# Result rows of a routed feed-forward added to the output by accumulating DMAs, in place of a read-back and sums on chip

## The reference

```python
x = x + tanh(g_xattn) * xattn(ctx, layernorm(x), mask, mask, ...)   # 8 heads, 16 blocks of 128 x 128
x = x + tanh(g_ffn)   * ffn(layernorm(x), w1, w2, w3, ...)          # 9 experts, top 2 of them per token
# ffn, with e over the 9 experts and cw[t, e] nonzero for two experts of each token t:
h   = silu(x_flat @ ew1[e].T) * (x_flat @ ew3[e].T)                 # 352 hidden columns
out = out + cw[:, e:e+1] * (h @ ew2[e].T)
```

## Time and profile before

| | |
|---|---|
| time, median of 3 runs | 218.54 us |
| profiled execution, its span (the profile gives no other time of it) | 234.1 us |
| PE busy | 205.4 us, 88% |
| DVE / ACT / POOL busy | 149.6 / 142.7 / 128.8 us |
| DMA | 34.91 MB, 149 GB/s on average |
| `y_rows` scatters on POOL (L616) | 38, mean 995 ns |
| `x_rows` scatters on POOL (L593) | 32, mean 1022 ns |

### The profile page before, as it was taken

One profiled execution on the slowest core, in us unless ns is written; L12 is line 12 of the kernel. 1 busy time (PEld: TensorE's weight loads), 2 busy tenths in 40 slices (PEclk: granted clock), 3 DMA queues, 4 the chain that ended last, 5 costly groups with the idle time before them and its releaser, 6 DMA issues.

```text
span 234.1 us, 5788 instructions
## 1 busy us (share of the span) xinstructions
PE 205.4 (88%) x1606; PEld 166.9 (71%) x1606; DVE 149.6 (64%) x523; ACT 142.7 (61%) x399; POOL 128.8 (55%) x230
## 2 busy tenths in 40 slices
PE   8999986999999999898883946299999999999981
PEld 3577653666666676565573945299999999999881
DVE  0469997788898698897865822344443444456774
ACT  2286869988778876786471620266667666666210
POOL 4237745132325876786783578556675756557320
PEclk9999999999999999999998897589999999999998
DMA  5999999999910100011372221121222221261194
GB/s 164 368 377 242 407 381 409 408 370 318 342 55 13 36 23 26 23 36 38 86 214 62 61 76 49 41 53 55 61 69 68 52 65 47 49 218 53 37 348 163
DMA packets 23602, 34.91 MB, mean 149 GB/s; under 512 B 2562, under 2 KB 15879, under 8 KB 23443
## 3 DMA queue, kind: packets, MB, share of 16 engines
q1 hardware_dynamic: 20610, 29.27, 37.9%
q0 software_dynamic: 2240, 4.23, 5.5%
q10 hardware_dynamic: 720, 1.02, 1.5%
HBM read 15.85 MB, written 19.06 MB: 149 GB/s over the span
## 4 chain that ended last, share of the span: by engine, by line
PE 56%; DVE 14%; another core or an unknown queue 7%; ACT 6%; DMA 6%; issue 5%; POOL 4%; SPq 1%; POOLq 0%; DVEq 0%; ACTq 0%
PE pt_ps L1363 10%; PE score_ps L1321 5%; PE pt_ps L1372 4%; PE score_ps L1323 4%; PE score_ps L1322 4%; PE score_ps L1176 4%; DMA kheads<-y_rows 3%; PE pt_ps L1116 3%; PE ps_a L1226 3%; PE pt_ps L1214 3%; PE score_ps L1126 2%; PE ps_b L1283 2%; DVE less L827 2%; ACT probs L401 2%
## 5 line engine op out<-in xcount | busy, mean ns | idle before, releaser
L616 POOL DMA_INDIRECT y_rows<-vals,ids x38 | 37.8, 995 | 17.2 <-ACT vals L473 9.6
L1363 PE MATMUL pt_ps<-w,probsT 128*128 x234 | 34.4, 285 | 14.6 <-ACT probsT L480 6.7
L1363 PEld LDWEIGHTS pt_ps<-w,probsT 128*128 128x128 f32 x234 | 32.1, 198 | 15.9 <-issue 15.8
L593 POOL DMA_INDIRECT x_rows<-stage,slot x32 | 32.7, 1022 | 10.4 <-issue 7.7
L401 ACT ACTIVATE probs<-score_ps,less 128x128 f32<-128x128 f32 x128 | 37.9, 419 | 0.4 <-DVE less L827 0.4
L1043 DVE TENSOR_TENSOR xg_low<-ps_a,xg_high 128x128 fp32r<-128x128 f32 x40 | 11.7, 291 | 37.1 <-issue 23.6
L473 ACT ACTIVATE vals<-pt_ps,xg 128x128 f32<-128x128 f32 x38 | 14.0, 368 | 34.4 <-PE pt_ps L1363 24.7
L1321 PE MATMUL score_ps<-w_high,xg_low 128*128 x80 | 30.3, 379 | 0.0
L1051 DVE TENSOR_TENSOR probs<-probs,score_ps 128x352 f32<-128x352 f32 x40 | 20.8, 521 | 11.2 <-PE score_ps L1323 5.3
L1323 PE MATMUL score_ps<-w_high,xg_high 128*128 x80 | 26.6, 332 | 0.0
L1322 PE MATMUL score_ps<-w_low,xg_high 128*128 x80 | 26.5, 332 | 0.0
(11 more groups left out here) (179 smaller groups left out, 445.6 us busy)
## 6 DMA issues: line engine op xcount, KB each, us to landing
x_rows<-pads SPq DMA_DIRECT2D x1, 9945.0 KB, 37.3
w_low<-in_w13T SPq DMA_DIRECT2D x3, 1056.0 KB, 11.0
xg<-x_rows SPq DMA_DIRECT2D x40, 65.0 KB
ctx_r<-in_ctxT SPq DMA_DIRECT2D x4, 512.0 KB, 7.7
y_rows<-pads SPq DMA_DIRECT2D x1, 2048.0 KB, 16.6
w<-in_w2T SPq DMA_DIRECT2D x1, 1728.0 KB, 11.2
kheads<-y_rows SPq DMA_DIRECT2D x3, 512.0 KB, 5.0
mask_b<-in_mask SPq DMA_DIRECT2D x4, 256.0 KB, 8.0
```

The source lines that it names most:

```text
L593: pool.indirect_dma_start(x_rows[:, :], bass.IndirectOffsetOnAxis(ap=slot[:, par, c, p:p + 1], axis=0), stage[:, par, c, p, :], None, boun ...
L616: pool.indirect_dma_start(y_rows[:, :], bass.IndirectOffsetOnAxis(ap=ids[:, s:s + 1], axis=0), yt[:, s, :], None, bounds_check=last_row, o ...
L1363: last = nc.tensor.matmul(into[:, 0:D], hidT[:, q3, c, :], w2[:, bass.ds(e3, 1), c, :].rearrange("p o d -> p (o d)"), start=(c == 0), stop ...
```

## The change

Results no longer go to `y_rows` with two rows per token. The output has 128 spare rows behind its 2048, and a second DRAM array `sums` has the same shape and begins at zero. The indirect DMA of an even tile adds its rows to `out`, which by then holds x2, and that of an odd tile adds to `sums`. Scatter k waits for the landing of scatter k-2, which went to the same array. After the last two have landed, one DMA issued by POOL adds `sums` to `out` in DRAM. All 40 tiles are scattered; the read-back, the one-hot matrices, the sums on chip and the stores at the end are gone. POOL's copy of the ids and the spacing writes are gone too: DVE writes the ids itself and limits them to a spare row of the own partition.

```diff
-SUMMED = 2
-BY_DVE, BY_POOL, BY_PE, ALL_PE = (0, 1), 2, 3, 4
+TURNS = 2
...
+        def scattered(t):
+
+            return t // TURNS * 16 + 16
...
-            sp.dma_start(y_rows.rearrange("(p n) d -> p n d", p=P), pads[:, 0:1, 0:D].to_broadcast([P, 2 * NB, D])).then_inc(st_zero, 16)
...
+            sp.dma_start(out[NB * P:(NB + 1) * P], pads[:, 0, 0:D]).then_inc(st_zero, 16)
+            sp.dma_start(sums.rearrange("(p n) d -> p n d", p=P), pads[:, 0:1, 0:D].to_broadcast([P, NB + 1, D])).then_inc(st_zero, 16)
...
-            sp.wait_ge(x2_stored, 16)
-            sp.wait_ge(ln2, NB)
-            sp.dma_start(xs[:], out_tok).then_inc(x2_back, 16)
...
-            for g, here in enumerate(PARTS):
-                sp.dma_start(ys[:, here, :, :], y_tok[:, here, :, :]).then_inc(ld_y[g], 16)
...
-            sp.wait_ge(st_out, 16 * len(PARTS))
+            sp.wait_ge(merged, 16)
...
-            nc.gpsimd.tensor_copy(pads[:, :, C_ID], part["nowhere"].to_broadcast([P, NE])).then_inc(pad_set, 1)
+            nc.gpsimd.memset(pads[:, :, C_ID:C_ID + 1], float(NOWHERE)).then_inc(pad_set, 1)
...
-            def tile(k, r):
-                s = k % YR
+            last_row = pool.to_reg((NB + 1) * P - 1)
+
+            def tile(k):
+                s, turn = k % YR, k % TURNS
+                if k == 0:
+                    pool.wait_ge(st_zero, TURNS * 16)
+                    pool.wait_ge(x2_stored, 16)
+                if k >= TURNS:
+                    pool.wait_ge(st_y[turn], scattered(k - TURNS))
                 pool.wait_ge(ids_cast, k + 1)
-                if k >= YR:
-                    pool.wait_ge(st_y[s], k // YR * 16)
-                nc.gpsimd.tensor_tensor(ids[:, s:s + 1], ids_in[:, s:s + 1], zero[:], ALU.add).then_inc(ids_copied, 1)
-                pool.wait_ge(ids_copied, k + 1)
-                if k == 0:
-                    pool.wait_ge(st_zero, 16)
-                if k < 3 * TR:
-                    short_space()
                 pool.wait_ge(y_done, k + 1)
-                pool.indirect_dma_start(y_rows[:, :], bass.IndirectOffsetOnAxis(ap=ids[:, s:s + 1], axis=0), yt[:, s, :], None,
-                                        bounds_check=last_row, oob_is_err=False).then_inc(st_y[s], 16)
+                pool.indirect_dma_start((out, sums)[turn][:, :], bass.IndirectOffsetOnAxis(ap=ids[:, s:s + 1], axis=0), yt[:, s, :], None,
+                                        bounds_check=last_row, oob_is_err=True, compute_op=ALU.add).then_inc(st_y[turn], 16)
...
-            for k in range(NT - SUMMED):
-                tile(k, k % TR)
+            for k in range(NT):
+                tile(k)
...
+            for n in range(TURNS):
+                pool.wait_ge(st_y[n], scattered(NT - TURNS + n))
+            whole, other = (t[0:NB * P].rearrange("(p n) d -> p (n d)", p=P) for t in (out, sums))
+            pool.dma_start(whole, other, accum_op=ALU.add, max_dma_last_dim=8192).then_inc(merged, 16)
...
                 if t >= YR:
-                    dve.wait_ge(ids_copied, t + 1 - YR)
-                nc.vector.tensor_copy(ids_in[:, t % YR:t % YR + 1], xg[:, place, C_ID:C_ID + 1]).then_inc(ids_cast, 1)
+                    dve.wait_ge(st_y[t % TURNS], scattered(t - YR))
+                nc.vector.tensor_scalar(ids[:, t % YR:t % YR + 1], xg[:, place, C_ID:C_ID + 1], part["nowhere"], None,
+                                        ALU.min).then_inc(ids_cast, 1)
```

More of the change, by code:

```diff
@@ L65, with build @@
 NCTX, WARM = 3, 24
-def build(nc, x, ctxT, mask, first, consts, row_consts, w_srcT, w_tgtT, w_outT, w13T, w2T, gateT, x_rows, y_rows, out):
+def build(nc, x, ctxT, mask, first, consts, row_consts, w_srcT, w_tgtT, w_outT, w13T, w2T, gateT, x_rows, sums, out):
     with ExitStack() as ctx:
@@ L95, in build @@
         share = sb("share", [P, P], BF16)
-        minus_half, minus_one, spare = sb("minus_half", [P, UN]), sb("minus_one", [P, UN]), sb("spare", [P, 3 * D], BF16)
+        minus_half, minus_one = sb("minus_half", [P, UN]), sb("minus_one", [P, UN])
         xs = sb("xs", [P, NB, D])
@@ L174, in build @@
         st_last = [sem(f"st_last{n}") for n in range(UN)]
-        st_y = [sem(f"st_y{n}") for n in range(YR)]
-        ld_y = [sem(f"ld_y{n}") for n in range(len(PARTS))]
-        x2_stored, x2_back, st_out = sem("x2_stored"), sem("x2_back"), sem("st_out")
+        st_y = [sem(f"st_y{n}") for n in range(TURNS)]
+        x2_stored, merged = sem("x2_stored"), sem("merged")
         dve_chain, act_chain, pool_set, table_chain = sem("dve_chain"), sem("act_chain"), sem("pool_set"), sem("table_chain")
@@ L300, in _ @@
                     sp.wait_ge(x2_done, NB * 2 - 1)
-                    sp.dma_start(out.rearrange("b t d -> t b d"), xs[:]).then_inc(x2_stored, 16)
+                    sp.dma_start(out[0:NB * P].rearrange("(b t) d -> t b d", b=NB), xs[:]).then_inc(x2_stored, 16)
                 sp.wait_ge(rows_known, n + 1)
@@ L471, in tile @@
                     if t >= YR:
-                        act.wait_ge(st_y[t % YR], t // YR * 16)
+                        act.wait_ge(st_y[t % TURNS], scattered(t - YR))
                     nc.scalar.activation(yt[:, t % YR, :], bank[1 if is_last(t) else 5][:, 0:D], ACT.Copy, scale=xg[:, place, C_WEIGHT:C_WEIGHT + 1]).then_inc(y_done, 1)
@@ L806, in weigh @@
                                                ALU.mult, ALU.mult).then_inc(weighed, 1)
-                nc.vector.tensor_scalar(stage[:, g % 2, :, :, C_ID], part["first_ids"].rearrange("p (c b) -> p c b", c=2), 2.0 * UN * P * g, None, ALU.add)
+                nc.vector.tensor_scalar(stage[:, g % 2, :, :, C_ID], part["first_ids"].rearrange("p (c b) -> p c b", c=2), float(UN * P * g), None, ALU.add)
                 assert route_links["weigh"] == LINKS["weigh"]
@@ L975, in _ @@
             table_counts(1)
[L977 to L987, removed]
-            def choose_rows(u, n):
-                here = slice(u * UN, (u + 1) * UN)
-                nc.vector.tensor_tensor(chosen_rows[:, n, here], part["rows_of"].unsqueeze(1).to_broadcast([P, UN, P]),
-                                        apart[:, n, here].unsqueeze(2).to_broadcast([P, UN, P]), ALU.is_equal).then_inc(row_chosen, 1)
             def cast_ids(t, place, turn):
@@ L1086, in _ @@
             tile_turns(tile, between)
-            for u in range(NB // UN):
-                choose_rows(u, 1)
-            dve.wait_ge(x2_back, 16)
-            for u in BY_DVE:
-                here = PARTS[u]
-                dve.wait_ge(summed, u + 1)
-                nc.vector.tensor_tensor(xs[:, here, :], sum_of(u), xs[:, here, :], ALU.add).then_inc(base_added, 1)
-            for g, here in enumerate(PARTS[:ALL_PE]):
-                base = xs[:, here, :]
-                if g in BY_DVE:
-                    dve.wait_ge(base_added, g + 1)
-                elif g == BY_POOL:
-                    dve.wait_ge(last_added, 1)
-                else:
-                    dve.wait_ge(summed, g + 1)
-                    base = sum_of(g)
-                dve.wait_ge(ld_y[g], 16)
-                nc.vector.tensor_tensor(xs[:, here, :], base, ys[:, here, 0, :], ALU.add).then_inc(y_added, 1)
-                dve.wait_ge(y_added, 2 * g + 1)
-                nc.vector.tensor_tensor(xs[:, here, :], xs[:, here, :], ys[:, here, 1, :], ALU.add).then_inc(y_added, 1)
-                dve.wait_ge(y_added, 2 * g + 2)
         @block.tensor
@@ L1387, in _ @@
             tile_turns(tile, between)
-            pe.wait_ge(ranks_kept, NG)
-            pe.wait_ge(hid_done, NT)
-            pe.wait_ge(x2_back, 16)
-            for u in (BY_PE, ALL_PE):
-                flat = xs[:, PARTS[u], :].rearrange("p b d -> p (b d)")
-                nc.tensor.matmul(sum_bank(u)[:, 0:flat.shape[1]], ident, flat, start=True, stop=False)
-            for u, part_of in enumerate(PARTS):
-                for n in range(SUMMED):
-                    pe.wait_ge(row_chosen, n * UN + part_of.start // UN + 1)
-                for b in range(part_of.start, part_of.stop):
-                    here = sum_bank(u)[:, (b - part_of.start) * D:(b - part_of.start + 1) * D]
-                    for n in range(SUMMED):
-                        if b == 0:
-                            pe.wait_ge(y_done, NT - SUMMED + n + 1)
-                        last = nc.tensor.matmul(here, chosen_rows[:, n, b, :], yt[:, (NT - SUMMED + n) % YR, :], start=(n == 0 and u < BY_PE),
-                                                stop=(n == SUMMED - 1 and (u < BY_PE or u == BY_PE and b == part_of.stop - 1)))
-                if u == ALL_PE:
-                    pe.wait_ge(ld_y[u], 16)
-                    for c in range(2):
-                        for b in range(part_of.start, part_of.stop):
-                            here = sum_bank(u)[:, (b - part_of.start) * D:(b - part_of.start + 1) * D]
-                            last = nc.tensor.matmul(here, ident, ys[:, b, c, :], start=False, stop=(c == 1 and b == part_of.stop - 1))
-                last.then_inc(summed, 1)
```

(14 more changed lines are left out.)

62 lines of the change are left out of this document (6 added, 56 removed).

## The result

The changed kernel takes 228.24 us (median of 4 runs, 227.06 to 230.34) against 218.21 us (4 runs, 216.70 to 218.61): a ratio of 1.0473 [1.0403, 1.0544]. It is slower by 10 us, where the forecast was 217.0 us and the range ended at 223.6. The profiled execution of the changed kernel took 227.43 us with a span of 225.6.

The account below looks back on a forecast made before the run. PE bounds the loop, then a 14.2 us tail; scatter 39 landing 223.78 + gap 0.28 + merge 7.7 + end 0.8 = 232.56 against 234.1, queue cost zero: gain 1.54, so 217.0 us from 218.54; range 213.2 to 223.6.

Parts of the forecast that it names:

- Scatters that wait for nothing follow each other at 1.28 us: POOL's tail: spacing of unhindered scatters, read from plain ones; put scatter 39's start at 220.78 us, after scatter 38 at 219.50.
- x: Extra landing time of an adding scatter over a plain one's 2.13 us: bounds 0 and 1.74, chosen 0.87, limit 1.07.
- P = (2.13 + 0.28 + x)/2: Scatter queue in the loop: price per scatter with two in flight; 1.64 us at x = 0.87, so cost zero.
- 1.74 us per scatter: Scatter queue: time available for each of 37 scatters, from 64.44 us between scatter 2 and scatter 39's natural start.
- POOL is not the bound in the loop: Expert-tile loop: claimed that removing POOL's id copies and spacing memsets gains nothing.
- Rival A: Scatter queue: the pair in flight is the bound; at x = 1.4 it ends 6.05 us late, 223.6 us; chance 0.32.
- The last 0.8 us: End of the kernel: time from the last landing to the end of the span, taken as 0.8 us.
- The merge: Final DMA adding `sums` to `out`: 1.95 us fixed plus 5.7 us data, 7.7 us, bounds 4.8 and 10.5.
- Rivals B and C: Merge length: B, all bytes paid, 10.5 us, 219.8 us, chance 0.14; C, one stream, 4.8 us, 214.1 us, chance 0.18.
- The stalls: Earlier profile's chain: five unexplained waits, 16.45 us in all, assumed absent from timed runs; without them span 217.65 us.
- The link from span to time: Whole kernel: the stall-free span of 217.65 us leaves 0.9 us around it to the median.
- the forecast's 12.67: Tail from the last result to the end: forecast 12.67 us, given among its signs as 12 to 13 us.

## Why the prediction was wrong

- **The step that failed: "Scatters that wait for nothing follow each other at 1.28 us".** The prediction took this from plain scatters and gave all of the addition's unknown cost, x, to the landing. So its price of a scatter in the queue, P = (2.13 + 0.28 + x)/2, has no floor of issue; POOL's own part was never bounded. It measured 1.855 us. By the prediction's own working 1.74 us per scatter were to be had (63.50 us for 37 in the changed kernel, 1.72), so 37 x 1.855 = 68.63 us come 5.13 late, and the waits for landings add 1.56: the 6.69 of the queue. "POOL is not the bound in the loop" fell with it.
- **x itself was near in size, but over its limit.** It measured 3.25 - 2.13 = 1.12 us; the prediction chose 0.87, with 1.07 as its limit. By its own formula 1.12 gives P = 1.765 us and a queue 0.87 us late, not 6.69. The pair in flight would allow (3.25 + 0.30)/2 = 1.78 us per scatter, which POOL's 1.855 covers. The limit of the pair was worked out, the limit of the issuer beside it was not.
- **Rival A was right in its place, not in its main cause or its price.** A late scatter queue and a merge long after ACT are what happened. But with four in flight only 1.5 us of scatter time come back, and sixteen in flight don't save the kernel before. A's 223.6 us was too low as it had no floor of issue. Its bound is there all the same, just under the issue: with scatters of 64 rows it takes over, and the formula, which counts every landing at the same length, doesn't hold the long ones that the waits show.
- **The last 0.8 us.** The prediction took the distance from SP's last landing to the end. In the changed kernel the last transfer is POOL's, and POOL's drain ends 3.0 us after it lands; with 0.2 more to the end of the span, that is 2.4 us too few. The rows of the drain stand in the trace before, with SP ending only just earlier; the prediction doesn't use them.
- **The merge was right in its sum, not in its parts**: 7.7 forecast, 7.9 measured. Its bytes moved for about 5.1 us (1.05 MB at 205 GB/s, the mean of the four full stretches, 172 to 229), where the forecast had 5.7, and the other 2.8 us stand against its 1.95. That the two errors nearly cancel is luck. Rivals B and C fall. By the Trainium skill, "Collectives: The Full Stack", section "The bandwidth ceiling: the fold count and why AG ≠ RS ≠ AR", an add reads two sources through one read ring and so runs at half the rate of a copy. The page tells this of collectives on a ring; the 248 GB/s for 16 engines is the prediction's estimate from it. In this case the trace agrees on the half: an 8 KB piece of the merge takes 629 ns on a DMA engine, one of POOL's plain copy 309 (medians). The estimate is a fifth above the measured 205, as a plain piece here moves at 8192/309 = 26.5 GB/s and not at the page's 31.
- **The stalls** of the earlier trace rows were rightly taken as that execution's own. Without them the last result was to be done at 219.89 - 16.45 = 203.44; it was at 203.04. The link from span to time was not right: in every run a time is 1.8 us longer than its span, where the prediction had 0.9. From the forecast's 217.0 to 228.24 the sum is then: tail +9.89, last result -0.40, 1.8 us around the span instead of 0.9, and a median 0.8 above the profiled execution.
- **Had the queue held**, the forecast would still have missed: the plain-scatter kernel is 2.3 us slower than before. Its tail is 3.0 us longer than the forecast's 12.67, 2.5 of them behind the landing of the merge, which stands with POOL's drain.

What stays open: what POOL does in the added 0.56 us of issue, why some landings are long, and what POOL's drain waits for. Only their durations were measured.

## What to carry to other kernels

An option on a transfer can cost the engine that issues it, not only the transfer: bound the issuer's time per instruction as well as the landing, and compare both with the time per tile. Where the two bounds lie close together, easing one brings up the other. An engine at 60% busy is no cover if it enters a loop with a backlog; what counts is its time per tile against the loop's period, times the tiles left. Before another engine is given the last transfer, read that engine's own end in the trace: a closing drain that ended level with the rest may come to stand alone.

## What the runs showed of the hardware

- An indirect scatter of 128 rows of 512 bytes keeps POOL for 0.97 to 1.00 us plain and 1.55 us adding (1.59 for the first); with 64 rows, adding, 1.41. Plain ones landed 2.13 and 2.24 us after their start, the last adding ones 3.2 to 3.4.
- POOL's closing drain takes 5.95 to 6.04 us when none of POOL's transfers is in flight, and in the kernel before ended 5.8 us after POOL's last operation; with a transfer of POOL's in flight it ended 2.8 to 3.1 us after that landed, in all seven kernels that end so.
- An adding DRAM-to-DRAM transfer of 1 MB, issued by POOL, lands 7.9 to 8.6 us after its start (8.8 in pieces of 2048), a plain one after 5.5. A piece of 8 KB takes 629 ns of a DMA engine adding and 309 plain.
